# A fused ViT tower on one core: the last tiles in another order, the zero fills at step 6, and identity multiplies in TensorE's pauses

## The chip, the cores and the metric

One core of one Trainium2 chip. The metric is the device time of one execution in microseconds (us). Before: 414.69 us, the median of three runs (413.27 to 414.73).

Engines: PE is TensorE, DVE VectorE, ACT ScalarE, POOL GpSimd, SP SyncE, which here only issues DMAs.

## What is computed

64 images, each 36 patches of 768 numbers and a class token, so 37 rows of 256 numbers per image, 2368 rows in all:

```python
z = layernorm(patches, ln1) @ W_proj + b_proj            # 768 -> 256
h = concat(cls, layernorm(z, ln2)) + pos_emb
h = h + attention(layernorm(h))                          # 37 rows per image, own row masked
y = layernorm(h)                                         # rows for the experts
probs = softmax(y @ router_w + router_b)                 # 8 experts
top 2 experts per row, their two gates normalised to 1
per expert: the 444 rows with the highest gates (capacity)
out_e = (gelu(y[tok] @ w1[e] + b1[e]) @ w2[e] + b2[e]) * gate
h + layernorm(sum over experts of out_e)
```

## The kernel before, in words

**The tile pipeline (0 to about 180 us).** 22 tiles (TILES) of three images, 111 rows. Each engine runs its own `step(i, slot)` for i = 0 to 27, and in step i an engine works on several tiles, each at another stage: z of tile i, the residual row and transposes of tile i - 1 or i - 2, attention of tile i - 2 or i - 3, x2 and scores of tile i - 4. What an engine does within a step, and in which order, is written out by hand; an engine takes its instructions in that order, and waits on semaphores (`need`, `plain`, `wait_ge`) hold all that stands behind them. Steps are unrolled at both ends and a loop in the middle.

**SP** in step i: loads x of tile i + 4 (L442, three DMAs; DVE's statistics L1080 read them in DVE's step i + 1), stores x2 of tile i - 4 (L487), at i == 18 the zero fills (L496, L498, L499: the first 2 of 46 blocks of 112 rows, one row of sums, and rows 112 to 127 of all 46 blocks), then stores tile i - 6 (L506 and L509). After the pipeline it loads the first expert's weights and stores the gates. All of these are on SP's one queue.

**ACT** in step i, as far as it matters: probT (L615), tT (L621), the residual row of tile i - 1 (L636), z's scaling for tile i (L641), scores of tile i - 4 (L654), x2 of tile i - 4 (L595), the exponential of tile i - 2 (L666), a copy (L671) and x1T of tile i - 1 (L677). PE needs the exponential for L900 and x1T for L805.

**POOL** in step i: one group of small operations makes the normalisations of up to three tiles together, k = 0 (z, tile i), k = 1 (h, tile i - 1), k = 2 (tile i - 4), L1607 to L1617; then L1624 adds the bias to tile i - 5, L1630 the positions to tile i.

**DVE** does statistics and, near the end, the choice of the best two experts and their gates, for tiles 0 to 15 within the pipeline and for 16 to 21 behind it (`best`, L1132 to L1145, `gates`, L1150 to L1162).

**Search and lists (about 188 to 231 us).** The gates are transposed on PE (L906 for 16 tiles, L912 for 6) into keys. Eight rounds (NR) find each expert's threshold: DVE counts (L1290, last round L1295) and makes `won`, one small PE matmul (L920) sums it, DVE makes the next candidate (L1301); ACT counts a part beside DVE (L710). Then positions (L922 to L927), the list of the first expert (L932), 24 calls of `keep_clock` (L939: an identity multiplied with itself into a PSUM bank that nobody reads), the gather of the first expert's rows by POOL (L1649), their transposes (L953) and the other lists (L944).

**Experts (about 231 to 413 us).** Eight experts on PE (L977 and L994), the rest beside it.

## Time and profile before

| | us |
|---|---|
| median of three runs | 414.69 |
| the profiled execution | 415.01 |
| its span, first to last instruction | 413.1 |
| PE busy | 348.5 (84%) |
| DVE busy | 315.5 (76%) |
| ACT busy | 255.3 (62%) |
| POOL busy | 224.1 (54%) |
| mean granted TensorE clock, share of full | 0.913 |

Busy shares are means over stages that have different limits, so each stage is read by itself: the slices of the page give the busy tenths of each engine and TensorE's granted clock over time, a timeline gives each instruction's start and duration, and in brackets how long its engine stood idle ahead of it and for whom. Times in the rows are us from the start of the span.

### The profile page before, as it was taken

Reading aid. Unit: us, or ns where it says so; the run is one execution under the profiler, and the core shown is the slowest. Engines: PE = TensorE matmul, PEld = TensorE weight load, DVE = VectorE, ACT = ScalarE, POOL = GpSimd, SP = SyncE. Lnnn points to the kernel's source line nnn. Section 1 sums busy time; section 2 is a strip of 40 time slices with the busy share of each in tenths; the row PEclk is TensorE's granted clock in tenths of the full one; section 3 lists DMA queues with packets and bytes.
Section 4 is the critical chain, followed back from the end, with each engine's and each line's share of the span. In section 5 each row is a group of like instructions: output and inputs, shape, how many; then the busy total and the mean of one; then the engine's idle time right before and its main releaser. Section 6 shows DMA issues by size and latency. Waiting matters only on the chain.

```text
span 413.1 us, 7904 instructions
## 1 busy us (share of the span) xinstructions
PE 348.5 (84%) x2128; PEld 307.3 (74%) x2128; DVE 315.5 (76%) x874; ACT 255.3 (62%) x552; POOL 224.1 (54%) x377
## 2 busy tenths in 40 slices
PE   2799999999999998731019899999999999999960
PEld 0499988878878886431009899999999999999950
DVE  6763788787878877679879755778888888787954
ACT  3263778767777785454710478677777776868620
POOL 3243676756667665340005443158686877755675
PEclk9896999999999999865555999999999999999995
DMA  6650114454444479768702496546758585852231
GB/s 185 173 115 12 35 55 110 136 154 129 138 141 129 122 123 108 186 198 268 20 0 68 119 274 190 161 151 179 216 173 236 166 235 169 250 169 64 60 84 45
DMA packets 49278, 57.29 MB, mean 139 GB/s; under 512 B 12248, under 2 KB 38229, under 8 KB 49244
## 3 DMA queue, kind: packets, MB, share of 16 engines
q1 hardware_dynamic: 42602, 43.11, 39.4%
q0 software_dynamic: 5568, 13.00, 11.8%
q10 hardware_dynamic: 1074, 0.79, 0.8%
q8 instruction: 14, 0.23, 0.2%
q14 instruction: 20, 0.16, 0.1%
HBM read 36.74 MB, written 21.36 MB: 141 GB/s over the span
## 4 chain that ended last, share of the span: by engine, by line
PE 60%; DVE 14%; issue 10%; POOL 8%; ACT 4%; DMA 1%; ACTq 1%; DVEq 1%; POOLq 0%
PE pall L994 18%; PE pz L977 17%; PE pall L837 6%; DVE wproj L1290 2%; PE pall L805 2%; POOL held L1630 2%; PE pall L812 2%; PE pall L939 2%; PE pall L1005 1%; ACT stage L576 1%; PE pz L785 1%; POOL nrm L1609 1%; PE pall L963 1%; DMA bproj<-in_b_proj 1%; PE pall L777 1%
## 5 line engine op out<-in xcount | busy, mean ns | idle before, releaser
L994 PE MATMUL pall<-halves 128*128 128x444 f32 x384 | 88.6, 365 | 1.9 <-DVE halves L1398 1.9
L977 PE MATMUL pz<-halves 128*128 128x444 f32 x384 | 87.1, 362 | 0.1
L994 PEld LDWEIGHTS pall<-halves 128*128 128x128 f32 x384 | 70.8, 188 | 7.0 <-issue 1.5
L977 PEld LDWEIGHTS pz<-halves 128*128 128x128 f32 x384 | 71.9, 188 | 5.1 <-DVE halves L1409 0.2
L1649 POOL DMA_INDIRECT held<-x_rows,gidx x32 | 36.9, 1152 | 58.8 <-DVE gidx L1339 38.2
L738 ACT ACTIVATE wproj<-pz,b1t 128x444 f32<-128x444 f32 x64 | 40.5, 633 | 44.0 <-PE pz L977 43.4
L1398 DVE TENSOR_TENSOR halves<-wproj,halves 128x444 fp32r<-128x444 f32 x64 | 39.7, 621 | 27.1 <-ACT halves L750 18.7
L837 PE MATMUL pall<-halves 128*112 128x256 f32 x396 | 56.1, 298 | 3.1 <-DVE halves L1089 3.1
L837 PEld LDWEIGHTS pall<-halves 128*112 128x112 f32 x396 | 51.2, 186 | 7.2 <-DVE halves L1089 3.5
L1673 POOL DMA_INDIRECT out<-rows,didx x28 | 37.0, 1323 | 22.1 <-DVE rows L1446 15.5
L750 ACT CAST halves<-wproj 128x444 fp32r<-128x444 f32 x64 | 36.1, 564 | 2.0
L1657 POOL DMA_INDIRECT rows<-sums,sidx x28 | 30.3, 1080 | 7.8 <-issue 7.5
L1368 DVE TENSOR_TENSOR halves<-stage,halves 128x512 fp32r<-128x512 f32 x32 | 22.0, 688 | 7.1 <-ACT halves L684 7.1
L636 ACT ACTIVATE x<-held,nrm 112x256 f32 (+1 forms) x22 | 13.2, 601 | 22.1 <-POOL nrm L1617 12.7
L576 ACT ACTIVATE stage<-stage,rs 112x768 f32<-112x768 f32 x22 | 22.6, 1027 | 6.9 <-POOL rs L1554 6.9
L805 PE MATMUL pall<-x1T,wq 128*128 128x112 f32 x176 | 25.0, 285 | 0.8 <-ACT x1T L677 0.3
L812 PE MATMUL pall<-wv,x1T 128*112 128x273 f32 x88 | 24.9, 406 | 0.0
L1607 POOL TENSOR_SCALAR nrm<-nmv 112x3 f32<-112x3 f32 (+2 forms) x26 | 6.2, 238 | 33.5 <-DVE nmv L1187 27.6
L1254 DVE BATCH_NORM_STATS2 hstat<-held 112x6 f32 (+1 forms) x22 | 9.4, 428 | 19.6 <-POOL held L1630 19.5
L805 PEld LDWEIGHTS pall<-x1T,wq 128*128 128x128 f32 x176 | 21.4, 191 | 3.3 <-ACT x1T L677 2.4
L1630 POOL TENSOR_TENSOR held<-held,posb 112x256 f32 (+1 forms) x22 | 16.0, 728 | 14.4 <-ACT held L641 14.4
L1080 DVE BATCH_NORM_STATS2 xstat<-stage 112x6 f32<-112x384 f32 x44 | 22.3, 548 | 1.7 <-DMA stage<-in_x 1.7
(283 smaller groups left out, 744.5 us busy)
## 6 DMA issues: line engine op xcount, KB each, us to landing
stage<-in_w SPq DMA_DIRECT2D x32, 512.0 KB
stage<-in_x SPq DMA_DIRECT2D x64, 108.0 KB
x_rows<-x SPq DMA_DIRECT2D x22, 224.0 KB, 2.9
x_rows<-held SPq DMA_DIRECT2D x22, 224.0 KB, 4.1
sums<-rows SPq DMA_DIRECT2D x7, 448.0 KB
out<-held SPq DMA_DIRECT2D x21, 111.0 KB
x_rows<-zero SPq DMA_DIRECT2D x1, 1474.9 KB
wproj<-in_w_proj ACTq DMA_DIRECT2D x1, 768.0 KB
```

The source lines that it names most:

```text
L576: nc.scalar.activation(xn, xin[:, slot, :], ACT.Identity, bias=rs[:, 0, 2:3], scale=rs[:, 0, 1:2]).then_inc(x_n, 1)
L738: nc.scalar.activation(hr[:, k % 2, 0:CAP], bank(k % 2)[:, 0:CAP], ACT.Gelu, bias=col(b1t, u)).then_inc(u_sb, 1)
L750: nc.scalar.copy(hh[:, k % 2, 0:CAP], hr[:, k % 2, 0:CAP]).then_inc(h_hi, 1)
L805: m = nc.tensor.matmul(bank(3)[:, o * P:(o + 1) * P], wqk[:, c, o * 128:(o + 1) * 128], xt_[:, c, :], start=(c == 0), stop=(c == EC - 1))
L812: m = nc.tensor.matmul(bank(4)[0:P, 0:VW], xt_[:, c, :], wv[:, c, :], start=(c == 0), stop=(c == EC - 1))
L837: nc.tensor.matmul(bank(2)[0:P, 0:ED], xs[:, c * P:(c + 1) * P], w[:, c, :], start=(c == k == 0), stop=False)
L977: m = nc.tensor.matmul(bank(k % 2)[:, 0:CAP], w[:, c, k * 128:(k + 1) * 128], xs[:, e % 2, c, 0:CAP], start=(n == 0), stop=(n == 3 * EC - 1))
L994: m = nc.tensor.matmul(pall[:, 2 * (e % 2) + o, 0:CAP], w[:, k, o * 128:(o + 1) * 128], hs[:, k % 2, 0:CAP], start=(k == 0 and n == 0), st ...
L1398: V_.tensor_tensor(hl[:, k % 2, 0:CAP], hr[:, k % 2, 0:CAP], hh[:, k % 2, 0:CAP].bitcast(fp32), ALU.subtract)\
L1649: pool.indirect_dma_start(xg[:, e % XB_N, j, :], None, x2_rows, bass.IndirectOffsetOnAxis(ap=gidx[:, k:k + 1], axis=0)).then_inc(g_in[e % ...
L1657: pool.indirect_dma_start(prev[:, j, :], None, sums[0:1 + e * SLOTS, :], bass.IndirectOffsetOnAxis(ap=sidx[:, k:k + 1], axis=0)).then_inc( ...
L1673: pool.indirect_dma_start(out, bass.IndirectOffsetOnAxis(ap=didx[0:n, k:k + 1], axis=0), final_of(e)[0:n, j, :], None, bounds_check=IMAGES ...
```

## The change

On SP the zero fills are issued in step 6 instead of step 18. In the last steps ACT, POOL and PE work in another order: on ACT z's scaling goes ahead of the residual row in step 21, and in step 22 the exponential and x1T go ahead of the scores and x2; on POOL the normalisation of tile 21's h is made by itself ahead of tile 18's in step 22, and the additions of L1624 of the last four tiles move (tile 18 and 19 to step 23, tiles 20 and 21 to step 26, behind a wait for the last gates, r_V). ACT's four casts of the first expert's weights leave the search rounds and stand behind them. `keep_clock` takes a bank and is called at many places between the steps from 22 on and the first gathered rows.

```diff
--- before.py
+++ after.py
@@ -491,7 +491,7 @@
                     load(c_l, b1t[:, :], b1)
                     sp.dma_start(b2t[:, :], b2.rearrange("a (k p) -> p (a k)", p=128),
                                  allow_slow_non_contiguous=True).then_inc(c_l, 16)
-                if isinstance(i, int) and i == 18:
+                if isinstance(i, int) and i == 6:
                     sp.wait_ge(s_xz, 5)
                     sp.dma_start(x2_blocks[0:P, 0:2, :], rep(zero[:, :].rearrange("p (a f) -> p a f", a=1), 1, 2))\
                         .then_inc(s_fill, 16)
@@ -630,15 +630,35 @@
                 t = i + 2
                 if live(t):
                     norm_x(t, (slot + 2) % 4)
-                t = i - 1
-                if live(t):
+                def residual_row(t):
                     plain(act, (x1T_ps, t - 1), (h_nb, t + 1))
                     nc.scalar.activation(x1[:, odd, :], tile_of(H, t), ACT.Identity, bias=norm(par, 2, 1),
                                          scale=norm(par, 1, 1)).then_inc(x1_ok, 1)
+
+                def turned(t):
+                    need(act, x1T_ps, t + 1)
+                    need(act, s_ps, t - 1)
+                    nc.scalar.copy(x1T[:, odd, :], bank(6)[:, 0:EC * P]).then_inc(x1T_sb, 1)
+
+                def exponentials(t):
+                    need(act, s_nmx, t + 1)
+                    need(act, pT_ps, t)
+                    need(act, g_h, t - 1)
+                    nc.scalar.activation(prob[:, :], masked[:, :], ACT.Exp, bias=nmax[:, 0:1], scale=1.0 / ED,
+                                         accum_out=psumr[:, par:par + 1]).then_inc(p_ok, 1)
+
+                last = isinstance(i, int) and i == TILES
+                if live(i - 1) and not (isinstance(i, int) and i == TILES - 1):
+                    residual_row(i - 1)
+                if last:
+                    exponentials(i - 2)
+                    turned(i - 1)
                 t = i
                 if live(t):
                     plain(act, (z_2, t + 1), (n_rs, i + 1))
                     nc.scalar.activation(tile_of(H, t), z2[:, :], ACT.Copy, scale=norm(par, 1, 0)).then_inc(z_sc, 1)
+                if isinstance(i, int) and i == TILES - 1:
+                    residual_row(i - 1)
                 if isinstance(i, int) and i == 1:
                     act.wait_ge(c_qk, 1)
                     nc.scalar.copy(wqk[:, :, :], bank(3)[:, 0:EC * ED].rearrange("p (c e) -> p c e", c=EC)).then_inc(c_tv, 1)
@@ -658,23 +678,15 @@
                     norm_row(i - 5, (slot + 3) % 4, odd)
                 if live(t) and not (isinstance(i, int) and i == TILES + 2):
                     norm_row(t, slot, par)
-                t = i - 2
-                if live(t):
-                    need(act, s_nmx, t + 1)
-                    need(act, pT_ps, t)
-                    need(act, g_h, t - 1)
-                    nc.scalar.activation(prob[:, :], masked[:, :], ACT.Exp, bias=nmax[:, 0:1], scale=1.0 / ED,
-                                         accum_out=psumr[:, par:par + 1]).then_inc(p_ok, 1)
+                if live(i - 2) and not last:
+                    exponentials(i - 2)
                 t = i - 2
                 if live(t):
                     plain(act, (h_dev, t + 1), (v_sb, t + 1))
                     nc.scalar.activation(tile_of(H, t, ED, HW), v[:, par, HW + 1:VW], ACT.Copy, scale=dev[:, odd:odd + 1])\
                         .then_inc(h_rw, 1)
-                t = i - 1
-                if live(t):
-                    need(act, x1T_ps, t + 1)
-                    need(act, s_ps, t - 1)
-                    nc.scalar.copy(x1T[:, odd, :], bank(6)[:, 0:EC * P]).then_inc(x1T_sb, 1)
+                if live(i - 1) and not last:
+                    turned(i - 1)
             pipeline(act, step, 6, 18)
 
             def w1_high(e, pr):
@@ -713,12 +725,13 @@
             act.wait_ge(r_odd, 1)
             for r in range(NR - 1):
                 signs_of(r)
-                if r >= 3:
-                    (w2_high if r % 2 == 0 else w1_high)(0, (r - 3) // 2)
 
             act.wait_ge(c_pool, 4)
             nc.scalar.copy(hitab[:, :, :], rep(iorow[:, 0:COLS].rearrange("p (c a) -> p c a", a=1), 2, 2)).then_inc(r_tab, 1)
             nc.scalar.copy(lotab[:, :, :], rep(locen[:, :].rearrange("p (c a) -> p c a", a=1), 2, 2)).then_inc(r_tab, 1)
+            for pr in range(2):
+                w1_high(0, pr)
+                w2_high(0, pr)
 
             act.wait_ge(c_l, N_L)
 
@@ -789,6 +802,11 @@
             turn_x(0)
             pe.wait_ge(c_dve, 2)
 
+            def keep_clock(n, b):
+
+                for _ in range(n):
+                    nc.tensor.matmul(bank(b)[:, 0:128], ident[:, :], ident[:, :], start=True, stop=True)
+
             def step(i, slot):
                 par = slot % 2
                 odd = 1 - par
@@ -838,6 +856,8 @@
                                              start=(c == k == 0), stop=False)
                     nc.tensor.matmul(bank(2)[0:P, 0:ED], ones2[:, :], zbias[:, :], start=False, stop=True)\
                         .then_inc(z_ps, 1)
+                if isinstance(i, int) and i >= TILES:
+                    keep_clock({TILES + 1: 5, TILES + 2: 3, TILES + 3: 8}.get(i, 0), 0)
                 t = i - 2
                 if live(t):
                     need(pe, x1_ok, t + 1)
@@ -893,6 +913,8 @@
                         m = nc.tensor.matmul(bank(4)[0:P, 3 * EC + EC * E:3 * EC + EC * E + E], bvrep[:, o, :], rwc[:, o, :],
                                              start=(o == 0), stop=(o == EC - 1))
                     m.then_inc(c_qk, 1)
+                if isinstance(i, int) and i >= TILES:
+                    keep_clock({TILES: 4, TILES + 1: 2}.get(i, 0), 0)
                 t = i - 3
                 if live(t):
                     need(pe, p_ok, t + 1)
@@ -906,6 +928,7 @@
                 m = nc.tensor.transpose(bank(t // 4)[:, t % 4 * P:(t % 4 + 1) * P], vrepa[:, t, :], ident[0:P, 0:P])
                 if t % 8 == 7:
                     m.then_inc(r_VT, 1)
+            keep_clock(24, 6)
             for t in range(TILES - EARLY):
                 if t % 3 == 0:
                     pe.wait_ge(r_rep, 2 + t // 3)
@@ -915,16 +938,20 @@
             pe.wait_ge(r_key, 3)
             pe.wait_ge(r_ka, 1)
             pe.wait_ge(c_pool, 4)
+            keep_clock(10, 7)
             for r in range(NR):
                 pe.wait_ge(r_won, r + 1)
                 nc.tensor.matmul(bank(r % 2)[:, 0:1], grp[:, :], won[:, :], start=True, stop=True).then_inc(r_n, 1)
+                keep_clock(9 if r < NR - 1 else 0, 7)
             pe.wait_ge(r_pick, 1)
             nc.tensor.matmul(bank(2)[0:P, 0:E], onesf[:, 0:P], thrrow[:, :], start=True, stop=True).then_inc(r_thr, 1)
+            keep_clock(2, 7)
             pe.wait_ge(r_ge, 1)
             gev = ge[:, :, :, :].rearrange("p e s t -> p (e s t)")
             n = 2 * E * TILES
             nc.tensor.matmul(bank(4)[0:P, 0:n], onesb[0:P, 0:P], gev, start=True, stop=True).then_inc(r_pos, 1)
             nc.tensor.matmul(bank(3)[0:P, 0:n], below[0:P, 0:P], gev, start=True, stop=True).then_inc(r_pos, 1)
+            keep_clock(17, 7)
             pe.wait_ge(r_first, 1)
             for q in range(TILES):
                 if q % (TILES // 2 + 1) == 0:
@@ -932,11 +959,6 @@
                 m = nc.tensor.matmul(bank(2)[0:P, 0:JT], ohlo0[:, q // 2, :, q % 2], ohval0[:, q // 2, :, q % 2],
                                      start=(q == 0), stop=(q == TILES - 1))
             m.then_inc(r_list, 1)
-
-            def keep_clock(n):
-
-                for _ in range(n):
-                    nc.tensor.matmul(bank(3)[:, 0:128], ident[:, :], ident[:, :], start=True, stop=True)
 
             def lists(h):
                 pe.wait_ge(r_val, h + 3)
@@ -1007,7 +1029,7 @@
                     if j % 2 or e == E - 1:
                         m.then_inc(y_ps, 1)
 
-            keep_clock(24)
+            keep_clock(16, 7)
             for h in range(2):
                 first_gathered(h)
                 lists(h)
@@ -1592,6 +1614,15 @@
             def step(i, slot):
                 par = slot % 2
                 on = [k for k, back in enumerate((0, 1, 4)) if live(i - back)]
+                if isinstance(i, int) and i == TILES:
+                    on = [2]
+                    pool.wait_ge(x1_ok, i - 2)
+                    pool.wait_ge(h_rw, i - 2)
+                    pool.wait_ge(h_mv, i)
+                    link(G.tensor_scalar(nrm[:, par, 0, 1:2], nmv[:, 1:2, 1], EPS, None, ALU.add))
+                    link(G.tensor_tensor(nrm[:, par, 1, 1:2], nrm[:, par, 0, 1:2], neghalf[:, :], ALU.pow))
+                    G.tensor_scalar(norm(par, 2, 1), nmv[:, 1, 0:1], norm(par, 1, 1), -1.0, ALU.mult, ALU.mult).then_inc(h_nb, 1)
+                    G.tensor_tensor(dev[:, par:par + 1], norm(par, 0, 1), norm(par, 1, 1), ALU.mult).then_inc(h_dev, 1)
                 if on:
                     last = isinstance(i, int) and i == TILES + 3
                     a, b = (1, 2) if last else (on[0], on[-1] + 1)
@@ -1616,8 +1647,11 @@
                             k = 1 if last else k
                             G.tensor_scalar(norm(par, 2, k), nmv[:, k, 0:1], norm(par, 1, k), -1.0, ALU.mult, ALU.mult)\
                                 .then_inc(done, 1)
-                for t in range(i - 6, i - 4) if isinstance(i, int) and i == TILES + 3 else (i - 5,):
-                    if live(t) and not (isinstance(i, int) and i == TILES + 2):
+                if isinstance(i, int) and i == TILES + 4:
+                    pool.wait_ge(r_V, 2)
+                for t in {TILES + 1: (i - 5, i - 4), TILES + 2: (), TILES + 3: (), TILES + 4: (i - 6, i - 5)}.get(i, (i - 5,)) \
+                        if isinstance(i, int) else (i - 5,):
+                    if live(t):
                         if isinstance(t, int) and t == 0:
                             pool.wait_ge(c_l, N_L)
                         need(pool, x2_ok, t + 1)
```

## Rows read from the trace of the kernel before

**Rows 1.** page, part 2: 40 slices, busy tenths and clock tenths

```profile
ACT  3263778767777785454710478677777776868620
...
PEclk9896999999999999865555999999999999999995
```

**Rows 2.** timeline of SP: start us, duration us, engine, line, operation

```profile
146.23 0.32 SPq L487 DMA_DIRECT2D x_rows<-x  x1
...
147.49 0.74 SPq L499 DMA_DIRECT2D x_rows<-zero  x1
148.27 0.79 SPq L506 DMA_DIRECT2D x_rows<-held  x1
149.11 3.87 SPq L509 DMA_DIRECT2D out<-held  x1
```

**Rows 3.** DMA view, 150 to 163 us, what all queues moved

```profile
DMA packets 624, 1.28 MB, mean 98 GB/s; under 512 B 0, under 2 KB 0, under 8 KB 624
```

**Rows 4.** DMA view, 149 to 165 us; last: us to landing

```profile
x_rows<-held SPq DMA_DIRECT2D x2, 224.0 KB, 16.3
```

**Rows 5.** DMA view, 60 to 80 us, same columns

```profile
x_rows<-held SPq DMA_DIRECT2D x2, 224.0 KB, 3.8
```

**Rows 6.** timeline of SP, about 69 us

```profile
68.81 0.35 SPq L487 DMA_DIRECT2D x_rows<-x  x1
...
70.09 1.22 SPq L442 DMA_DIRECT2D stage<-in_x  x3
```

**Rows 7.** timelines of DVE and ACT, 78 to 82 us

```profile
78.92 1.01 DVE L1080 BATCH_NORM_STATS2 xstat<-stage 112x6 f32<-112x384 f32 x2
...
80.25 0.14 DVE L1241 SCALAR_TENSOR_TENSOR nmax<-v,nm 112x1 f32<-112x1 f32 x1
...
81.15 0.37 ACT L666 ACTIVATE prob<-masked,nmax 112x112 f32<-112x112 f32 x1
```

**Rows 8.** timeline of PE, 23 to 38 us, 18 matmuls each

```profile
23.65 2.34 PE L837 MATMUL pall<-halves 128*112 128x256 f32 x18
...
32.97 4.16 PE L837 MATMUL pall<-halves 128*112 128x256 f32 x18
```

**Rows 9.** PE by stretch: us, busy (count), clock, DMA share, GB/s

```profile
167.50:171.00 3.50, 1.73 (x11) 0.98 0.69 186
171.00:174.40 3.40, 3.40 (x12) 0.52 0.64 177
```

**Rows 10.** timelines of ACT, PE and DVE, 167 to 175 us

```profile
167.86 0.60 ACT L636 ACTIVATE x<-held,nrm 112x256 f32<-112x256 f32 x1 [1.87 <-POOL nrm L1617]
...
169.99 1.31 PE L805 MATMUL pall<-x1T,wq 128*128 128x112 f32 x8
...
174.68 0.14 DVE L1241 SCALAR_TENSOR_TENSOR nmax<-v,nm 112x1 f32<-112x1 f32 x1
```

**Rows 11.** timelines of POOL and DVE, 180 to 184 us

```profile
180.21 2.10 POOL L1624 TENSOR_TENSOR held<-held,lnb 112x256 f32<-112x256 f32 x3
...
180.26 0.74 DVE L1132 TENSOR_TENSOR LG<-LG,rbb 112x48 f32<-112x48 f32 x1 [1.52 <-ACT LG L654]
...
181.72 0.65 DVE L1136 TENSOR_TENSOR eqm<-eqm,erev 112x48 f32<-112x48 f32 x1
...
183.67 0.21 DVE L1136 TENSOR_TENSOR eqm<-eqm,erev 112x48 f32<-112x48 f32 x1
```

**Rows 12.** by line, 187 to 212 us: busy, mean ns, idle before

```profile
L920 PE MATMUL pz<-won,grp 128*128 128x1 bf16 x8 | 1.5, 183 | 20.7 <-DVE won L1293 17.4 <-DVE won L1297 3.3
```

**Rows 13.** timeline of PE, 222 to 225.5, then 225.5 to 228 us

```profile
221.65 4.10 PE L939 MATMUL pall<-ident 128*128 128x128 f32 x19
...
225.27 2.71 PE L939 MATMUL pall<-ident 128*128 128x128 f32 x22
```

**Rows 14.** timeline of PE; all engines by stretch, last DMA share, GB/s

```profile
229.34 0.58 PE L953 MATMUL pz<-ident,held 112*128 112x112 f32 x4
...
228.50:229.00 0.50, 0.50 (x13) 0.50 (x11) 0.04 (x1) 0.43 (x1) 0.00 (x0) 1.00 0.13 45
```

## The prediction

> **What bounds the kernel now.** I read the page's slices first [rows 1]: TensorE's granted clock is full (2.4 GHz) through the tile pipeline (to about 170 us), at half (1.2 GHz) from about 178 to 226 us (search, lists, first gather), and full through the experts. Then the timeline of each engine. The pipeline is one chain per tile of some 6.2 us in which PE, DVE, ACT and POOL hand on to each other; PE hardly pauses, so a tile that comes late is not made up later. From 177 to 230 us DVE is the chain, and PE waits for it. After that PE is the bound, 21 us for each expert, and nothing there changes: what the change wins or loses ahead of 231 us moves the end by as much. The profiled execution took 415.01 us, 1.9 beyond its span of 413.1 and 0.3 above the median of the three runs (414.69); I sum against 415.0.
>
> **SP: the zero fills move from step 18 to step 6.** This is the largest term. In the kernel before, the last tile of x has been asked for when the big fill is issued (147.49) [rows 2], so nobody needs the queue soon. The big fill is 46 blocks of 16 rows, 736 pieces of 2052 bytes. From 150 to 163 us the queue moved nothing under 2 KB, so nothing but fill: 624 packets, 98 GB/s [rows 3]. That is 48 packets per us, 15.3 us for 736. Stores issued behind it landed after 16.3 us in the median [rows 4] instead of 3.8 [rows 5], and SP itself was held for some 3.9 us at each issue from 149.11 on [rows 2]. So this queue works in order, and all of SP's transfers stand in it.
> At step 6 the fills come right behind the store of tile 2's x (68.81) and ahead of the loads of x for tile 11, which were issued at 70.09 [rows 6]. The fill was issued 147.49 - 146.23 = 1.3 us behind such a store [rows 2], so now at 70.1. The next store landed 148.27 + 16.3 - 147.49 = 17.1 us after the fill's issue, so now at 87.2. Behind it stand a store of 111 rows of 1 KB and three loads of 36 x 768 numbers (108 KB), 0.43 MB; at 177 GB/s, a rate of this queue with nothing slow in it [rows 9], that is 2.4 us, and I add 0.3 to the signal: x of tile 11 is there at 89.9. Counted by SP's own issues it is the same: 71.7 + 4 x 3.9 = 87.3 for the last issue, and at least 2 us to landing.
> DVE reads it at 78.92 [rows 7]. DVE takes its work in order, so it stands for 89.9 - 78.92 = 11.0 us, with the row maximum of tile 6 behind it, for which ACT's exponential waits, and with that PE. The slack on that path is small: the maximum was ready at 80.25 + 0.14 = 80.39 and used at 81.15 [rows 7], 0.8 us. Behind the exponential ACT's copy of x1T has no other cover, as PE took it up within 0.1 us. So 10.2 us. Bounds: 7.5, if the loads land as early as the store ahead of them (87.2); 11.5, if the last is only issued at 87.3 and takes 3.8 us.
> PE stands for 10 us in this, and its clock falls, as it did at 171 us behind a stretch in which PE was busy for 1.73 of 3.5 us [rows 9]. What that costs: the same 18 matmuls took 4.16 us at half clock and 2.34 at full [rows 8]. Bounds 1.8 (one such block) and 3.4 (two); I take 2.5, as a step has one such block and as much again of other matmuls. **Together 12.7 us lost, between 9.3 and 14.9.**
> The Trainium skill has a rule here ("SBUF — State Buffer", Door 1: The DMA port swizzle): how fast a DMA goes depends on how many of the 16 SBUF ports its partitions reach; 16 neighbouring partitions reach 4 of them, a quarter of 436 GB/s. The measured 98 GB/s agrees with its 109, and it says that the fill is as slow at any step. By its figure the fill alone would be 13.9 us instead of 15.3, and the sum 1.4 less.
> What the old place gives back: I find nobody in the tail who waits for a store or for the experts' first weights, so 0.
>
> **The reordering of the last tiles.** POOL now makes the normalisation of tile 21 alone instead of together with that of tile 18, whose statistics are done later, and with one column instead of two. ACT waited 1.87 us for it at 167.86 [rows 10]; bounds 0 and 1.87, I take 1.0, as the statistics of tile 21 no longer wait for another tile's, and two of POOL's operations move behind the one that ACT waits for. ACT then runs the exponential of tile 20 and the copy of x1T of tile 21 ahead of the scores and x2 of tile 18 (two activations that PE does not wait for). PE's block at 169.99 [rows 10] starts about 1.0 us earlier; the five identity multiplies ahead of the transposes take up what more there was.
> Doing z's scaling ahead of the residual row in step 21 costs 0, as the residual waits for POOL there too; bounds 0 and 0.6, one such activation [rows 10].
> POOL's additions of the last tiles (L1624) move behind the final gates. Before, three of them, 2.10 us from 180.21, lay beside DVE's best-expert operations: L1132 took 0.74, L1136 0.65, and L1136 of the second pass, with POOL still, 0.21 [rows 11]. With L1135 (0.38 against 0.21) that is 0.5 + 0.17 + 0.44 = **1.1 us won**; bounds 0.4 (L1136 alone) and 1.1. Two additions (1.4 us) now fall into the start of the search. The one DVE operation there that might meet them is keysa (0.62), which starts sooner than POOL can be told of the gates: 0, bounds 0 and 1.4.
> The Trainium skill ("SBUF — State Buffer", SBUF: two separate sides) says that DVE and POOL take turns at a shared port pair, held for a whole instruction, for DVE operations with two SBUF inputs or in a two-port mode. The trace agrees (0.65 against 0.21). By that rule keysa would lose up to 0.7 if POOL came first, and the sum would be 0.7 more.
> ACT's four casts of the first weights leave the search and stand behind it; in its slices ACT is all but idle from 207 to 227 us [rows 1]: 0.
>
> **The identity multiplies.** One call is two records. At half clock 19 records took 4.10 us and at full 22 took 2.71 [rows 13]: 0.43 and 0.24 us a call. Nine calls are 2.2 us and fit into a pause of a search round (17.4 us for seven of the eight, 2.5 each [rows 12]); the 24 behind the first transposes are 5.8 us and end about when the last tiles' copies are ready, hidden by DVE by some 0.3; the ten ahead of round 0 end with DVE's first count: 0.1 us lost.
> What a full clock is worth: from 171.0 to 174.4 PE was busy throughout at half clock [rows 9], on the chain to the maximum at 174.68 [rows 10]: 1.7 us at the most, 0 at the least. I take 1.5. From there to the last tile's scores DVE is the chain (it makes the gates of the first 16 tiles in between), so nothing more. In the search and list stage PE's part is eight matmuls of 183 ns [rows 12] and three larger ones; bounds 0 and 0.09 x 8 + 0.6 = 1.3, I take 0.3, because a single small matmul is mostly time through the array. The 22 small matmuls of the first list are hidden by DVE. At the gather the last rows' packets ended before 229.0 and PE came at 229.34 because its keep-clock calls had run at half clock [rows 14]: 0.4 won.
> **Won together 1.0 + 1.1 + 1.5 + 0.3 + 0.4 - 0.1 = 4.2 us,** between 1 and 5.5.
>
> **Sum.** 415.0 + 12.7 - 4.2 = 423.5 us. Ends: 415.0 + 9.3 - 5.5 = 418.8 and 415.0 + 14.9 - 1 = 428.9.
>
> **Rivals.** (A) The loads are not held up: packets of loads pass or share with those of the fill, since they run from HBM to SBUF and the fill the other way. Then only the gains stay, 415.0 - 4.2 = 410.8, faster. It decides the sign from the point at which x of tile 11 lands before about 83 us. For it: only stores were seen behind the fill, no load. Against it: 13 us in which not one other packet moved [rows 3], and SP held at each issue [rows 2]. 0.10.
> (B) They are held up in part (5 us of stall, 1.8 of clock): 415.0 + 6.8 - 4.2 = 417.6. 0.05.
> (C) The identity multiplies don't hold the clock. Then they are in the way: nine calls at half clock are 3.9 us in a pause of 2.5, 1.4 us more for each round, or the 24 calls run to 10.3 us and hold the transposes up by some 4. For it: the last round of the search has 9 calls in a pause of 3.3 us [rows 12], and the clock fell at 171 with PE busy for half of the time. Against it: in the other rounds 2.2 of 2.5 us is far more than that 1.73 of 3.5 [rows 9]. One such fall, with the stall as forecast: 423.5 + 3 = 426.5. 0.15.
> The forecast has 0.70.
>
> **How the numbers follow.** The range reaches from (B) to the forecast's upper side with (C) in it, 417 to 428; left out are (A) and what lies beyond the ends. 0.5% is about what a measurement of this kernel can tell from no change, 2.1 us. Faster by more: (A), 0.10. Within it: the edge of (B), 0.03. Slower: 0.87.
>
> **What the profile would show.** DVE's statistics of tile 11 (L1080) with a wait of 8 to 11 us for stage<-in_x near 79 us, packets of 2052 bytes alone from 71 to 87, PE idle for 10 us and some digits of 5 in its clock behind; if there is none, (A). In the tail: PE's L805 of tile 21, counted from the last z, 1 us sooner; no POOL beside L1136; PEclk at 9 to 230 us, or (C); rounds of the search at 2.6 us still. The prediction is wrong if the loads of tile 11 land on time.

## The result and the profile after

The changed kernel takes 427.04 us (median of six runs, 426.05 to 428.99), the kernel before 414.06 (six runs, 413.21 to 415.46): ratio 1.0321, interval 1.0286 to 1.0355. That is 13.0 us slower. I had forecast 423.5 with a range of 417 to 428: sign and range held, the time lies 3.5 us over the forecast. The profiled execution took 428.80 us, its span 426.8.

| | before | after |
|---|---|---|
| span, us | 413.1 | 426.8 |
| PE busy, us | 348.5 | 374.3 |
| DVE busy, us | 315.5 | 315.2 |
| mean granted TensorE clock | 0.913 | 0.946 |

TensorE has more to do (the identity multiplies), the others the same: all the loss is waiting. The page's slices of after, 10.7 us each, to lay beside [rows 1]:

```profile
PE   2799999519999999989876699999999999999970
...
PEclk9798999957999999999999699999999999999995
```

There are two holes: from 75 to 107 us, with PE at 5 and 1 and then the clock at 5 and 7, and from 235 to 245 us, with the clock at 6. Between them the clock is full through the whole search, where it was at half before. The first hole was forecast, the second was not.

**The first hole.** SP's timeline, then the DMA view of 72 to 85 us, then all engines by stretch (busy and count of PE, PEld, DVE, ACT, POOL; clock, DMA share, GB/s):

```profile
68.62 0.61 SPq L499 DMA_DIRECT2D x_rows<-zero  x1
69.28 0.93 SPq L506 DMA_DIRECT2D x_rows<-held  x1
70.26 3.86 SPq L509 DMA_DIRECT2D out<-held  x1
74.16 12.44 SPq L442 DMA_DIRECT2D stage<-in_x  x3
...
DMA packets 622, 1.28 MB, mean 98 GB/s; under 512 B 0, under 2 KB 0, under 8 KB 622
...
86.00:87.00 1.00, 0.00 (x0) 0.00 (x0) 0.00 (x0) 0.00 (x0) 0.00 (x0) 0.50 0.60 86
87.00:88.00 1.00, 0.00 (x0) 0.00 (x0) 0.00 (x0) 0.00 (x0) 0.00 (x0) 0.50 0.92 258
```

The fill runs as in [rows 3], at 98 GB/s with nothing beside it, until 87 us, and SP is held for 12.4 us at the three loads of tile 11. Then the timelines of DVE, ACT and PE, which answer [rows 7]:

```profile
92.51 1.02 DVE L1102 BATCH_NORM_STATS2 xstat<-stage 112x6 f32<-112x384 f32 x2 [14.94 <-DMA stage<-in_x]
...
93.99 0.39 ACT L647 ACTIVATE prob<-masked,nmax 112x112 f32<-112x112 f32 x1 [14.18 <-DVE nmax L1263]
...
94.52 0.44 PE L922 MATMUL pall<-ident,prob 112*112 112x112 f32 x1 [13.78 <-ACT prob L647]
...
103.71 0.26 PE L922 MATMUL pall<-ident,prob 112*112 112x112 f32 x1
...
109.83 0.26 PE L922 MATMUL pall<-ident,prob 112*112 112x112 f32 x1
```

This is the mechanism of the forecast, instruction by instruction, but 14.94 us long and not 11.0.

**The second hole.** The chain of waits, in order of time (start, us, what ran):

```profile
200.43 1.38 SPq L517
...
203.48 1.74 SPq L450
...
205.26 6.45 SPq L450
...
212.74 19.11 DMA x_rows<-gate
...
232.10 0.96 issue
233.06 1.23 POOL held L1683
```

L450 stores the gates, L1683 is the first gather (L1649 before). Its indices were ready at 229.8 us, and it was issued at 233.06: it waited for the gates to land. The DMA view of 223 to 231 us, and PE's timeline to the experts ("ident" with "ident" is the identity multiply; each call is two records):

```profile
DMA packets 1, 0.02 MB, mean 2 GB/s; under 512 B 0, under 2 KB 0, under 8 KB 0
...
228.32 3.82 PE L808 MATMUL pall<-ident 128*128 128x128 f32 x32
236.66 0.41 PE L975 MATMUL pall<-ident,held 112*128 112x112 f32 x2 [4.53 <-DMA held<-x_rows,gidx]
238.80 0.64 PE L975 MATMUL pall<-ident,held 112*128 112x112 f32 x2 [1.73 <-DMA held<-x_rows,gidx]
239.23 2.22 PE L966 MATMUL pall<-ohvals,rows 112*112 112x64 bf16 x22
...
244.08 4.12 PE L999 MATMUL pz<-halves 128*128 128x444 f32 x12
```

Every gate had been moved by 223 us; the landing came at 231.9. The Trainium skill ("Perfetto Trace Analysis", DMA Instruction — HWDGE) says that the last descriptor of a DMA signals only once the data write is confirmed, which can be "surprisingly long" where the target is HBM. The trace agrees: 9 us. Then PE stands for 4.53 and 1.73 us, its granted clock goes from 1.00 (232 to 236 us) to 0.50 (239 to 246 us), and the lists take 2.22 us each. Before's, at full clock:

```profile
228.20 1.31 PE L944 MATMUL pall<-ohvals,rows 112*112 112x64 bf16 x22
```

**Where the 13.7 us of span come from.** The prologue (what runs ahead of the first tile) differs from execution to execution: the first row maximum (nmax, L1241 before) starts between 38.5 and 42.4 us over the profiled executions. So I count from it. All starts in us after the first row maximum; "wait" is from the start of the indices (gidx) to the first gather, "rest" from the gather to the span's end:

| | last row maximum | indices | first gather | wait | rest | end of span |
|---|---|---|---|---|---|---|
| before | 132.2 | 177.6 | 178.1 | 0.5 | 192.6 | 370.7 |
| after | 144.4 | 188.7 | 192.1 | 3.4 | 193.8 | 385.9 |
| e1, fill back | 129.4 | 173.9 | 179.9 | 6.0 | 194.5 | 374.3 |
| e2, fill alone | 146.2 | 192.1 | 193.6 | 1.5 | 194.5 | 388.1 |
| e3, order alone | 129.2 | 174.3 | 177.0 | 2.7 | 192.6 | 369.6 |
| e4, multiplies alone | 130.8 | 177.6 | 179.4 | 1.8 | 194.1 | 373.4 |
| e6, weights and gates first | 129.4 | 173.9 | 177.7 | 3.8 | 193.4 | 371.1 |
| e7, fill on ACT's queue | 135.7 | 181.6 | 183.4 | 1.8 | 193.8 | 377.2 |
| e8, half the fill | 135.5 | 180.0 | 184.0 | 4.0 | 193.2 | 377.2 |
| e9, slices | 129.3 | 174.1 | 178.1 | 4.0 | 193.1 | 371.2 |
| e10, slices, gates early | 129.4 | 174.0 | 174.5 | 0.5 | 194.1 | 368.6 |
| e11, before, gates early | 130.7 | 197.4 | 197.8 | 0.5 | 192.5 | 390.3 |
| e13, after, gates early | 144.0 | 188.5 | 189.0 | 0.5 | 194.0 | 383.0 |
| e14, e10 with more calls | 129.4 | 173.7 | 174.2 | 0.5 | 194.0 | 368.2 |

In the column of the last row maximum after is 12.2 us behind before, at the indices 11.1, at the gather 14.0, at the end 15.2; its prologue was 1.5 us shorter, which makes the 13.7. Medians are over several runs and are compared by ratios below; a single trace stands up to 3.4 us from its own median (e3: 412.12 against 415.47).

### The profile page after: what moved, and what is told of

Its sections match the earlier page's. It is cut to its first block, busy times and chain, and to the rows that moved or that the text cites. A ratio compares the mean times of both kernels' runs of the same rounds, so it can differ in the third digit from the quotient of the medians.

```text
span 426.8 us, 8425 instructions
## 1 busy us (share of the span) xinstructions
PE 374.3 (88%) x2388; PEld 335.4 (79%) x2388; DVE 315.2 (74%) x874; ACT 256.3 (60%) x552; POOL 225.7 (53%) x379
## 4 chain that ended last, share of the span: by engine, by line
PE 58%; issue 9%; DVE 9%; DMA 8%; POOL 7%; SPq 4%; ACT 3%; DVEq 0%; POOLq 0%; ACTq 0%
PE pz L999 17%; PE pall L1016 17%; PE pall L855 6%; DMA x_rows<-gate 4%; PE pall L823 3%; DMA stage<-in_x 2%; PE pall L830 2%; SPq L450 2%; PE pz L798 2%; POOL held L1664 2%; PE pall L1027 1%; SPq L442 1%; PE pall L985 1%; POOL nrm L1640 1%; PE pall L790 1%
## 5 line engine op out<-in xcount | busy, mean ns | idle before, releaser
L999 PE MATMUL pz<-halves 128*128 128x444 f32 x384 | 88.6, 367 | 0.0
L999 PEld LDWEIGHTS pz<-halves 128*128 128x128 f32 x384 | 73.2, 191 | 5.0
L1683 POOL DMA_INDIRECT held<-x_rows,gidx x32 | 36.4, 1138 | 55.9 <-issue 42.2
L1707 POOL DMA_INDIRECT out<-rows,didx x28 | 37.1, 1324 | 21.7 <-DVE rows L1468 15.2
L808 PE MATMUL pall<-ident 128*128 128x128 f32 x264 | 32.1, 278 | 0.8 <-DVE scratch L1300 0.8
L808 PEld LDWEIGHTS pall<-ident 128*128 128x128 f32 x264 | 30.5, 192 | 1.0 <-DVE scratch L1300 1.0
```

The lines of the kernel that those rows point to most:

```text
L808: nc.tensor.matmul(bank(b)[:, 0:128], ident[:, :], ident[:, :], start=True, stop=True)
L999: m = nc.tensor.matmul(bank(k % 2)[:, 0:CAP], w[:, c, k * 128:(k + 1) * 128], xs[:, e % 2, c, 0:CAP], start=(n == 0), stop=(n == 3 * EC - 1))
L1683: pool.indirect_dma_start(xg[:, e % XB_N, j, :], None, x2_rows, bass.IndirectOffsetOnAxis(ap=gidx[:, k:k + 1], axis=0)).then_inc(g_in[e % ...
L1707: pool.indirect_dma_start(out, bass.IndirectOffsetOnAxis(ap=didx[0:n, k:k + 1], axis=0), final_of(e)[0:n, j, :], None, bounds_check=IMAGES ...
```

## The experiments

**e1: the fill back at step 18, all else as changed.**

```diff
-                if isinstance(i, int) and i == 6:
+                if isinstance(i, int) and i == 18:
```

> The changed kernel with the zero fills at step 18 again and all else as changed. Theory: in the changed kernel's trace every tile from the stalled one on came 15.1 us later against the kernel before than the tiles ahead of it, so the fill's place costs 15.1 us, and what remains is the tail: the last tiles 3.1 us sooner (reordering and full clock), then some 3 us lost at the first gather to the stores of the gates, which now stand behind the last stores of h, and 1.1 us of lists at half clock. 427.0 - 15.1 = 411.9 us. Rival (my prediction as it stood: fill 12.7, tail gains of 4.2 and no new wait): 427.0 - 12.7 = 414.3 us. Second rival: the wait for the gates was only a matter of the fill having moved; then the wait and the fall of the clock are gone, 408 us.

Measured: 416.88 us against 415.26 of before beside it, ratio 1.0030 (0.9988 to 1.0071). So the place of the fill costs 1.0321 - 1.0030 = 2.9%, 12.1 us, close to the first rival's 12.7 and under my 15.1. The rest of the change wins nothing that the interval tells, and the theory's 411.9 us is missed, though the table shows e1 3.7 us ahead at the indices. The gather's timeline:

```profile
220.67 2.34 POOL L1683 DMA_INDIRECT held<-x_rows,gidx  x1 [36.40 <-issue]
```

6.0 us behind its indices, which is worse than in after. The second rival falls: the wait isn't made by the fill's move.

**e2: the kernel before with the fill at step 6 alone** (the same line, the other way).

> The kernel before with one edit: the zero fills are issued in step 6 instead of 18. Theory: 15.1 us more, 414.1 + 15.1 = 429.2 us, with DVE's wait for x of tile 11 of some 14 us and the same tail as before. The prediction's step gave 12.7: 426.8 us. A rival in which the reordered tail has a part in the loss would leave this one under 425 us.

Measured: 427.24 us, ratio 1.0295 (1.0238 to 1.0352): 12.2 us, the same as from e1. Its DVE waited as after's did:

```profile
92.00 1.02 DVE L1080 BATCH_NORM_STATS2 xstat<-stage 112x6 f32<-112x384 f32 x2 [15.33 <-DMA stage<-in_x]
```

The fill's place is nearly the whole of the 13.0 us, with or without the rest. My theory's 429.2 us was too high; the 426.8 us of the prediction is the nearer.

**e3: the reordering alone** (ACT, POOL and the casts as changed, fill at 18, identity multiplies as before).

```diff
-                    keep_clock({TILES + 1: 5, TILES + 2: 3, TILES + 3: 8}.get(i, 0), 0)
...
-                    keep_clock({TILES: 4, TILES + 1: 2}.get(i, 0), 0)
...
-            keep_clock(16, 7)
+            keep_clock(24, 3)
```

> The kernel before with the reordering alone (ACT, POOL and the casts); the fills at step 18, no identity multiplies but the 24 that were there. Theory: 1 us won in the last tiles and 1.1 us at the choice of the best experts, but the stores of the gates issued behind the last additions hold the first gather up by some 3 us: 415 us, about no change (414 to 416). Rival (no wait for the gates): 414.1 - 2.1 = 412.0 us.

Measured: 415.47 us, ratio 1.0002 (0.9962 to 1.0042), as the theory had it. In the table it is 3.0 us ahead at the last row maximum and 3.3 at the indices, and loses 2.2 of it to the wait:

```profile
217.57 1.23 POOL L1674 DMA_INDIRECT held<-x_rows,gidx  x1 [33.41 <-issue]
```

**e4: the identity multiplies alone** (TensorE's part of the change, nothing else).

> The kernel before with the identity multiplies alone: same counts and places on TensorE, nothing else changed. Theory: the clock stays full from the last tiles to the first gather, as in the changed kernel up to 237 us; it wins what my sum gave for it, 1.5 + 0.3 + 0.4 - 0.1 = 2.1 us: 412.0 us, with the search rounds at 2.6 us as before. Rival: the full clock is worth nothing ahead of the experts, as DVE is the chain there: 414 us. Second rival: without the reordering the counts don't fit and the clock falls or the calls stand in the way: over 415 us.

Measured: 414.81 us, ratio 1.0010 (0.9978 to 1.0043): the rival's 414. It is 1.4 us ahead at the last row maximum, as I had it (1.5), and level at the indices. PE's and DVE's timelines at the start of the search:

```profile
183.53 4.12 PE L795 MATMUL pall<-ident 128*128 128x128 f32 x20 [0.87 <-DVE scratch L1287]
187.49 0.17 PE L931 MATMUL pz<-won,grp 128*128 128x1 bf16 x1
...
187.70 0.16 DVE L1310 SCALAR_TENSOR_TENSOR cand<-pz,rest 128x1 int32<-128x1 int32 x1 [1.80 <-PE pz L931]
```

The ten calls ran for 4.12 us, at half clock (2.4 at full), and DVE stood for 1.80 us behind them. This is my rival (C), once. In after the same ten calls ran at full and hid. Behind the gather 1.5 us more went (rest 194.1 against 192.6).

**e6: the weights and the gates issued on SP ahead of the last two stores of h**, on e1.

```diff
+                if isinstance(i, int) and i == TILES + 4:
...
+                    for h in range(2):
+                        load_w1(0, h)
+                        load_w2(0, h)
+                    for a, b, n in ((0, EARLY, 1), (EARLY, TILES, 2)):
+                        sp.wait_ge(r_V, n)
+                        store_gates(a, b)
                 t = i - 6
```

> The changed kernel with the fills at step 18, and with the loads of the first expert's weights and the stores of the gates issued ahead of SP's last two stores of h instead of behind them. Theory: in the run with the fills back the first gather stood 6.0 us behind its indices (214.69 to 220.67) and waited for the stores of the gates, which SP issued behind everything else; the wait and with it the fall of the clock at the gather (17 us at half) go, -5.5 and -1.4 us against that kernel's 416.9: 410 us, faster than the kernel before by 1.0 to 1.5%, the gather 0.5 us behind its indices. Rival: what is late is the 16 queues' work as a whole, 2 MB of weights and 5000 packets of 4 bytes, and the order at its end is of no matter: 415 to 417 us. Second rival: POOL's gather comes as soon as it can, but something else is then late by the same time (the weights): 414 us.

Measured: 415.10 us against 414.60, ratio 1.0023 (0.9991 to 1.0054): the rival's 415 to 417. The wait shrank from 6.0 to 3.8 us only, and changed its name, in the chain of waits:

```profile
198.46 1.05 SPq L531
...
199.88 16.94 DMA x_rows<-held
...
216.97 0.96 issue
```

Now the two stores of h come last, behind the 5,000 packets of 4 bytes. Swapping the order at the end of a full queue moved the wait to the next store.

**e7: the big fill on ACT's queue, in ACT's step 5.**

```diff
+                if isinstance(i, int) and i == 5:
+                    act.wait_ge(s_xz, 5)
+                    nc.scalar.dma_start(x2_blocks[P:128, :, :],
```

> The changed kernel with the big fill issued from ACT, on ACT's queue, in ACT's step 5 instead of on SP's in step 6. Theory: the loads of x are late because they stand behind the fill in one queue that works in order; on another queue they pass it, so DVE's wait for x is under 2 us and the time is 427.0 - 15 = 412 us. Rival: the fill holds the 16 DMA engines themselves (2052 bytes of 16 neighbouring rows at a time), so loads of any queue crawl beside it: DVE's wait is 7 us or more, 419 us and over. ACT may stand for its issue by up to 4 us, which the trace would show on ACT.

Measured: 419.58 us (two runs), ratio 1.0120 (1.0044 to 1.0197): the rival's time, with a wait somewhat under its 7 us. The DMA view of 62 to 72 us, then SP, then DVE:

```profile
DMA packets 477, 0.98 MB, mean 98 GB/s; under 512 B 0, under 2 KB 0, under 8 KB 477
## 3 DMA queue, kind: packets, MB, share of 16 engines
q10 hardware_dynamic: 477, 0.98, 92.5%
...
60.32 12.61 SPq L442 DMA_DIRECT2D stage<-in_x  x3
...
76.11 1.02 DVE L1104 BATCH_NORM_STATS2 xstat<-stage 112x6 f32<-112x384 f32 x2 [6.16 <-DMA stage<-in_x]
```

q10 is ACT's queue, q1 SP's. In ten us q1 moved not one packet, though SP stood at its loads for 12.6 us. So my reason fell: it isn't only one queue's order, the fill keeps SP's queue off the DMA engines from ACT's queue too. That the wait is 6.16 us and not 14.94 doesn't show what the other queue is worth, for the fill also moved in time: ACT issued it at 56.24 us, SP in after at 68.62, which is 11 us sooner counted from the first row maximum, and SP's loads of tile 10 now stood right behind one store. From the fill's issue to the statistics that DVE was late with it is 19.9 us here (to 76.11) and 23.9 in after (to 92.51); the rest of the gain is the earlier start. A run with ACT's queue at the old moment is missing. The Trainium skill ("DMA: Bandwidth & Descriptors", Queues, rings and completion order) says that an engine takes its queues in turn, a packet of at most 64 descriptors at a time. It calls 9 to 17 typical. The fill has 736 / 16 = 46 pieces for each engine; this trace agrees with the rule only if those 46 go as one packet, which no run shows.

**e8: 23 of the 46 blocks in step 6, the others in step 18.**

```diff
-                    sp.dma_start(x2_blocks[P:128, :, :],
+                    sp.dma_start(x2_blocks[P:128, 0:23, :],
```

> The changed kernel with 23 of the 46 blocks filled in step 6 and the other 23 in step 18. Theory: the fill moves 48 pieces per us, so half of it holds the loads up by 7.7 us less: DVE's wait for x of tile 11 is 14.9 - 7.7 = 7.2 us, TensorE's clock still falls behind it, 419.5 us, less up to 1.5 us if it doesn't fall. Rival (a fixed price of a stall, or a queue that is full at any size of fill): over 424 us. Second rival (slack in the loads greater than I think): wait under 4 us, 415 us.

Measured: 419.79 us (two runs), ratio 1.0125 (1.0051 to 1.0200), forecast 419.5. DVE's wait, forecast 7.2:

```profile
83.96 1.02 DVE L1105 BATCH_NORM_STATS2 xstat<-stage 112x6 f32<-112x384 f32 x2 [6.87 <-DMA stage<-in_x]
```

Half the fill takes 8.1 us off the wait, for 7.7 expected: the price goes with the number of pieces.

**e9: the big fill in six slices of up to 8 blocks, in steps 3 to 8.**

```diff
+                if isinstance(i, int) and 3 <= i <= 8:
+                    b0 = 8 * (i - 3)
+                    b1_ = min(b0 + 8, Q + 2)
+                    sp.dma_start(x2_blocks[P:128, b0:b1_, :],
```

> The changed kernel with the big fill in six slices of 8 (the last of 6) blocks in steps 3 to 8. In the kernel before the DMA engines are busy for 0.33 to 0.53 of these steps of 5.8 us; a slice of 128 pieces is 2.7 us, 0.46 of a step. Theory: it fits, no load is later than DVE wants it by over 1 us, and the whole 15 us of the fill are hidden; and the tail of SP's queue is free of it too, so the first gather's wait is the 3 us of the changed kernel and not the 6 of the run with the fills back: 413 to 414 us. Rival: backlog grows from slice to slice and DVE stands at tile 11 or 12 for 3 us or more, with the clock falling: 417 us or more.

Measured: 412.24 us, ratio 0.9973 (0.9936 to 1.0010). DVE's only waits for x from 50 to 100 us:

```profile
75.24 1.02 DVE L1105 BATCH_NORM_STATS2 xstat<-stage 112x6 f32<-112x384 f32 x2 [0.17 <-DMA stage<-in_x]
...
82.00 1.02 DVE L1105 BATCH_NORM_STATS2 xstat<-stage 112x6 f32<-112x384 f32 x2 [0.39 <-DMA stage<-in_x]
```

The same bytes in the same part of the kernel make DVE wait 0.6 us instead of 15. The gather still waits 4.0 us. e9 differs from e1 only in where and in what pieces the fill goes, and their last row maxima lie level (129.3 and 129.4), yet e9's ratio is 0.57% lower, 2.4 us: its last gates were issued 4.3 us sooner, counted from the first row maximum, and its gather came 1.8 us sooner. So the fill at step 18 does load SP's queue to the end of the tail (the two intervals just overlap).

**e10: e9, and the gates of the first 16 tiles stored at SP's step 24, those of the last six ahead of the last stores of h, the weights behind.**

```diff
+                if isinstance(i, int) and i in (TILES + 2, TILES + 4):
+                    sp.wait_ge(r_V, 1 if i == TILES + 2 else 2)
+                    store_gates(*((0, EARLY) if i == TILES + 2 else (EARLY, TILES)))
```

> The kernel with the fill in slices, and besides the stores of the gates moved on SP: those of the first 16 tiles to step 24, as soon as their gates are made, those of the last six ahead of the last two stores of h; the weights stay behind. Theory: in the runs so far the first gather came 0.96 us behind the landing of SP's last small stores, and these landed some 9 us after their last packet of 4 bytes, whatever the place of the fill; with the 16 tiles' part gone before, the last packets are written by about 190 us, all has landed before the indices are there (about 212 us), the gather is issued 0.5 us behind them instead of 4, and TensorE's clock doesn't fall in the pause: 412.2 - 3.7 - 1.2 = 407.4 us, ratio 0.983 to the kernel before. Rival: the clock falls at the gather all the same, since the pause from the indices to the first rows is 8 us and the multiplies at full clock don't cover it: 408.6 us. Second rival: no wait but a later one takes its place (weights): 411 us and over.

Measured: 410.99 us against 415.52, ratio 0.9901 (0.9868 to 0.9934): 1% faster than before, though not the 0.983 of the theory. POOL, then PE:

```profile
214.76 1.83 POOL L1686 DMA_INDIRECT held<-x_rows,gidx  x1 [31.00 <-DVE gidx L1364]
...
219.00 0.55 PE L978 MATMUL pall<-ident,held 112*128 112x112 f32 x2 [2.25 <-DMA held<-x_rows,gidx]
...
220.79 2.22 PE L969 MATMUL pall<-ohvals,rows 112*112 112x64 bf16 x22
```

The gather waits for its indices alone, 3.6 us sooner than in e9. But the lists still run at half clock, and "rest" is 1.0 us longer than in e9: by the ratios 3.0 us were won of the 4.9 forecast. The first rival was right on the clock.

**e11: the kernel before with the same move of the gates.**

> The kernel before with the same move of the stores of the gates and nothing else. Theory: before, the gather was issued 0.47 us behind its indices, so it waited for no store; no change, ratio 0.998 to 1.002. Rival: before stood at the edge, and in many executions the gates were late there too; then this is faster by 1 us or more, 0.997 or less.

Measured: 432.25 us, ratio 1.0415 (1.0359 to 1.0472), missed by both. ACT and DVE in the search:

```profile
216.44 0.62 ACT L684 CAST halves<-stage 128x512 fp32r<-128x512 f32 x1 [22.19 <-DMA stage<-in_w]
...
218.43 0.22 DVE L1293 TENSOR_SCALAR won<-cnt,signs 128x1 bf16<-128x1 f32 x1 [21.04 <-ACT junka L710]
```

The kernel before casts the first weights between ACT's counts. The weights now came late, and with them the search stood for 21 us. The same move in e13 and e10, whose casts stand behind the search, makes no such wait: the casts' move, which I had put at 0, is what lets SP's order be changed. What e11 was to tell, whether before's gates were late in some executions, it can't.

**e13: the changed kernel with the same move of the gates.**

> The changed kernel (fills at step 6) with the same move of the stores of the gates alone. Theory: of the 13.0 us that the change lost, 3.0 are the first gather's wait for the gates and 1.1 the lists at half clock behind it: 427.0 - 4.1 = 422.9 us, 1.020 to the kernel before; the gather is 0.5 us behind its indices. Rival (the trace's wait is not what sets the end, or the clock falls anyway): 425 us or more.

Measured: 426.13 us, ratio 1.0269 (1.0217 to 1.0320), against 1.0321 of after: about 0.5%, 2.2 us, though the intervals overlap. The forecast of 422.9 us is missed; it is the rival's "425 us or more".

```profile
228.91 1.82 POOL L1683 DMA_INDIRECT held<-x_rows,gidx  x1 [30.92 <-DVE gidx L1361]
```

The gather is 3.2 us sooner in the table (189.0 against 192.1), as expected; the 1.1 us of the lists didn't come, since they stay at half clock.

**e14: e10 with 13 calls instead of 9 ahead of the last round, and 26 instead of 16 behind the first list.**

```diff
-                keep_clock(9 if r < NR - 1 else 0, 7)
+                keep_clock({NR - 2: 13, NR - 1: 0}.get(r, 9), 7)
...
-            keep_clock(16, 7)
+            keep_clock(26, 7)
```

> The kernel with the slices and the moved gates, with more identity multiplies in the two pauses ahead of which its clock fell: 13 calls instead of 9 ahead of the search's last round, and 26 instead of 16 behind the first list. Theory: what lets the clock fall is TensorE's standing still (1.22 us in the last round, then 2.25 us for the first gathered rows); ten calls are 2.4 us at full clock, so the stand is gone, the clock stays full to the experts, the two lists take 1.3 us each instead of 2.2 and the first twelve multiplies of the experts 2.7 instead of 4.2: 411.0 - 2.5 = 408.5 us, ratio 0.984 to the kernel before. Rival: the clock falls for another reason than the stands (the many small multiplies of the lists); then no change or, with the calls at half clock in the way of the first rows, 1 us slower.

Measured: 409.25 us against 415.23, ratio 0.9875 (0.9834 to 0.9917). PE's timeline:

```profile
218.69 0.41 PE L978 MATMUL pall<-ident,held 112*128 112x112 f32 x2
220.00 0.41 PE L978 MATMUL pall<-ident,held 112*128 112x112 f32 x2 [0.91 <-DMA held<-x_rows,gidx]
220.25 1.31 PE L969 MATMUL pall<-ohvals,rows 112*112 112x64 bf16 x22
...
223.22 0.64 PE L978 MATMUL pz<-ident,held 112*128 112x112 f32 x2 [1.20 <-DMA held<-x_rows,gidx]
223.65 2.22 PE L969 MATMUL pall<-ohvals,rows 112*112 112x64 bf16 x22
```

The forecast was 0.984. The first list now takes 1.31 us, so the stand ahead of the first rows was what cost the clock there. It fell later, behind the pauses of 0.91 and 1.20 us between the rows. Whether e14 beats e10 isn't settled (the intervals overlap, the traces differ by 0.4 us); both beat the kernel before.

## Why the prediction was right or wrong

**The fill: right in kind; right in sum partly by luck.** I summed 12.7 us; e1 and e2 give 12.1 and 12.2. Inside, DVE stood 14.94 us and not 11.0, PE 13.8 and not 10.2 (over my upper bound of 11.5). After's first six row maxima started 1.5 us sooner than before's, those from the eleventh to the nineteenth 13.7 us later: a jump of 15.1. PE's stand is 13.8 of it, which leaves 1.3 for the clock instead of 2.5. That 1.3 is only what was left: PE's one step at half clock (from its transpose of prob at 94.52 us to the next at 103.71) took 9.2 us and the full-clock step behind it 6.1, so the fall cost 3.1 us, near my upper bound of 3.4. About 1.8 of it was made up, as before's own steps in this place are 6.5 and 7.0 us long, with pauses; I had written that a late tile isn't made up. The jump of 15.1 became 12.1 in the time because some 3 us came back in the tail, which I had put at 0 (next paragraph): two errors that cancel. The failed step is the landing: I let the next store land at 87.2 and gave the loads 2.7 us more. The slow stretch lasted to 87 us; the store issued at 69.28 landed after 19.8 us, at 89.1, not after 16.3; and the loads followed at 92.4, since the 196 to 271 GB/s behind the fill moved some 1.3 MB in these 5.4 us and not my 0.43: the stores and loads issued behind them were carried as well (an inference from the rate and SP's issues). The slack was 14.94 - 13.78 = 1.2 us, not 0.8.

**What the old place gives back: not 0.** From e1 to after, 15.0 us at the last row maximum shrink to 12.3 at the gather, because e1's gather waited 6.0 us for SP and after's 3.4. The times of e1 and e9 say 2.4 us for the same (see e9). So "I find nobody in the tail who waits for a store" hid this term too. Its size is open: e3, also with the fill at 18, waited only 2.7 us.

**The gains: this is the step that failed.** I forecast 4.2 us; e1 against before gives -1.2 (between -2.9 and +0.5). It isn't that the edits don't work:
- The reordering was undersized up to the gates: 3.0 us at the last row maximum (e3) for my 1.0. In e3 the clock stayed full (1.00) up to that row maximum at 169.8 us without one added multiply, and fell to 0.50 only from 172 us, so the 1.5 us that I gave the clock came with the order too; together they give 2.8 (e1), not the sum of 3.0 and 1.4 (e4).
- The contention is gone: DVE's operations beside which POOL's additions lay in [rows 11] take 0.21 us each in after. But from the last row maximum to the indices e3 gains only 0.3 us (45.1 for 45.4), not my 1.1. Two of the gate operations of the first 16 tiles now lie beside a moved pair of additions and take 0.70 and 0.32 us, which I had not looked at.
- The rounds stay at 2.6 us, as said, and the clock is full through the search in after: (C) did not happen there. It did in e4.
- "I find nobody in the tail who waits for a store" is the false sentence. POOL's first gather waits for every store of x2, h and the gates. Before, it was issued 0.5 us behind its indices, so no row of idle time showed a wait; how near it was, the old trace did tell (the stores of the last gates, with their time to landing):

```profile
L450 SPq DMA_DIRECT2D x_rows<-gate x2: 612/1190/1768, 199.2 to 199.8; - x2
...
DMA to landing us min/median/max: 12.4/14.0/15.6
```

  The last one landed 15.6 us behind its issue at 199.8, at about 215.4; the indices were ready at 220.0, so the slack was 4.6 us in this execution. In e1 to e4 and e7 to e9 the same landing came 18 to 21 us behind its issue. In e3 the last gates were issued at the same moment as before (157.5 us behind the first row maximum), landed 2.7 us later, and the indices were 3.3 us earlier: together 6.0 for a slack of 4.6, and the gather was issued 1.2 us behind the landing. Why the landing took 18 us and more where before shows 15.6 is open, and whether other executions of before were late too. Even e2 and e4, without the reordering, wait 1.0 and 1.3 us more than it; with the indices 3 us earlier and SP's last stores held behind POOL's postponed additions it is 2.2 (e3), 2.9 (after) and 5.5 (e1).
- "At the gather 0.4 won" is the other one. Before, 24 calls, most of them at half clock, had covered the whole pause from 219.6 to 227.8 us; the 16 of after at full clock end 4.5 us early (2.9 of these are the gather's own longer wait; in e10, without it, 2.25 are left), PE stands, and the clock falls just ahead of real work. The lists (2.22 us for 1.31, twice) and the first experts' multiplies (4.12 for 2.67) then run at half. That is 3.3 us of longer work in after; the column "rest" gives what is left of it: 193.1 to 194.5 us in every kernel with the added multiplies, 192.5 or 192.6 in before, e3 and e11, so 0.5 to 1.9 us. The difference is what my "0.4 won" saw a part of: PE took up the first rows 3.6 us behind the gather's issue in after, and 7.3 us behind it in before, where the calls still ran. And the added multiplies aren't the only cause of a fall: e2, without them, has 194.5, with its second list at half clock behind a pause of 0.91 us between its rows, and e3 fell too, behind a pause of 0.95 us (its first twelve multiplies of the experts take 3.94 us). Of the kernels without them only before and e11 kept the clock full.

**Rivals.** (A) and (B) are refuted, and e7 shows that on another queue the loads are held up as well. (C) I gave 0.15 and a place in the search; it came at the gather, at 1.2 us in after ("rest") for the 3 us that I gave it, by a mechanism that I had the rows for [rows 13, 14] and read the wrong way round.

**Sum again, by ratios of two separate runs:** 414.1 + 12.2 (fill, e2) + 1.2 (the rest, e1) = 427.5, measured 427.04. (The 12.1 of e1 would prove nothing here, as it is itself the difference of after and e1.)

## What to carry to other kernels

Before moving a large DMA of few partitions, ask whose loads stand behind it within its own length, on any queue; cut into slices that fit the idle share of each step, the same bytes cost 0.6 us of waiting instead of 15 (e9). When a chain is shortened, list all that its end waits for, also the waits that show no idle time yet: a store that lands some us ahead of its reader is the next bound, and its signal can come 9 us behind its last packet (after). Its landing can be read from the old trace even where nobody waits for it. And multiplies that keep the clock must be counted at the speed at which they will then run, or they end before the pause does.

## What the runs showed that I had not expected

- A DMA of 736 pieces of 2052 bytes on 16 rows, on ACT's queue, left SP's queue not one packet for 10 us (e7), at 98 GB/s in all.
- 5,000 packets of 4 bytes (the gates) signalled 9 us after the last of them had been moved, with the DMA engines idle in between (after), and in e6 a store behind them on the queue landed only 16.9 us after its issue.
- The traces differ by up to 3.9 us before the first tile is through (38.5 to 42.4 us to the first row maximum; one trace for each kernel; ahead of that point only the first slice of e9, e10 and e14 is an edit), so traces are best compared from a point behind the prologue.
